# Edge layers of a graph network on one core: five more tiles fetched by indirect DMA, and twelve instead of six fetched tiles completed by VectorE

## The reference

```python
e = edge_attr @ We + be
m = jax.nn.relu(x[src] + e)
agg = jax.ops.segment_sum(m, dst, num_segments=x.shape[0])
h = ((1.0 + eps) * x + agg) @ W1 + b1
# batch norm over the nodes, relu
return jax.nn.relu(h @ W2 + b2)
```

## Time and profile before

| | |
|---|---|
| median of 3 runs | 876.57 us (871.54 to 879.27) |
| the profiled execution: its own time | 878.66 us |
| the profiled execution: its span, first to last instruction | 876.9 us |
| TensorE busy (matmul) | 786.6 us, 90% |
| VectorE busy | 697.3 us, 80% |
| ScalarE busy | 543.0 us, 62% |
| GpSimd busy | 283.1 us, 32% |
| mean granted TensorE clock | 0.965 |

### The profile page before, as it was taken

The page is one execution under the profiler, slowest core; times in us unless marked ns, Lnnn a source line. Parts: engine busy times, 40 slices in busy tenths (PEclk is TensorE's granted clock), DMA queues, the critical chain, the costliest instruction groups (busy, mean ns, idle before and its releaser), DMA issues.

```text
span 876.9 us, 12030 instructions
## 1 busy us (share of the span) xinstructions
PE 786.6 (90%) x3566; PEld 601.8 (69%) x3566; DVE 697.3 (80%) x1253; ACT 543.0 (62%) x1034; POOL 283.1 (32%) x230
## 2 busy tenths in 40 slices
PE   2979899899889899979999999988999989999895
PEld 2667565477467668756777777776777867878674
DVE  7989856799966968886798878977889778997635
ACT  2288213566563423556797778877788677864656
POOL 3000387877300000016760067400863028610000
PEclk9989999799989999997999999999999999999998
DMA  5323246788472330417994199823996249942001
GB/s 117 103 80 107 69 131 195 227 248 243 150 261 85 118 131 1 154 39 178 215 223 120 35 222 222 206 92 84 225 221 161 86 126 215 220 105 65 32 6 54
DMA packets 61329, 122.12 MB, mean 139 GB/s; under 512 B 9096, under 2 KB 22698, under 8 KB 61269
## 3 DMA queue, kind: packets, MB, share of 16 engines
q0 software_dynamic: 22096, 52.18, 27.2%
q1 hardware_dynamic: 39173, 69.17, 25.1%
HBM read 105.60 MB, written 15.73 MB: 138 GB/s over the span
## 4 chain that ended last, share of the span: by engine, by line
PE 59%; DVE 21%; ACT 11%; DMA 6%; issue 3%; SPq 0%; ACTq 0%; DVEq 0%
PE ps L712 12%; PE ps L1043 9%; PE ps L1082 6%; PE ps L1026 6%; PE ps L1067 6%; DVE z_parts L1955 5%; PE ps L820 5%; DMA onehot_dst<-onehot_rows 4%; PE ps L965 3%; PE ps L911 3%; DVE gathered_parts L1702 2%; DVE w L1462 2%; PE ps L704 2%; ACT slot_recs L1146 2%; ACT queued L1298 2%
## 5 line engine op out<-in xcount | busy, mean ns | idle before, releaser
L680 POOL DMA_INDIRECT queued<-node_rows,srci x92 | 144.4, 1569 | 198.3 <-DMA node_rows<-work 152.1
L1043 PE MATMUL ps<-z_parts,onehot_dst 128*125 128x512 f32 x664 | 189.4, 397 | 2.9 <-DMA onehot_dst<-onehot_rows 2.6
L1955 DVE SCALAR_TENSOR_TENSOR z_parts<-ps,z_parts 128x512 fp32r<-128x512 f32 x216 | 146.0, 689 | 34.5 <-ACT z_parts L1354 30.0
L712 PE MATMUL ps<-w,xT 128*125 128x512 f32 x660 | 169.2, 409 | 3.7 <-DVE w L1462 2.7
L1354 ACT ACTIVATE z_parts<-ps 128x512 fp32r<-128x512 f32 x216 | 128.1, 598 | 49.8 <-PE ps L1026 44.6
L712 PEld LDWEIGHTS ps<-w,xT 128*125 128x125 f32 x660 | 125.0, 193 | 35.1 <-issue 5.7
L1043 PEld LDWEIGHTS ps<-z_parts,onehot_dst 128*125 128x125 f32 x664 | 121.0, 186 | 39.9 <-issue 11.5
L1026 PE MATMUL ps<-x_parts,gather_lhs 128*128 x408 | 130.5, 401 | 5.1 <-DVE z_parts L1955 5.1
L1026 PEld LDWEIGHTS ps<-x_parts,gather_lhs 128*128 128x128 f32 x408 | 76.9, 189 | 26.0 <-issue 8.0
L674 POOL DMA_INDIRECT gathered<-rel_rows,rowi x75 | 77.8, 1037 | 22.8 <-issue 22.2
L1955 DVE SCALAR_TENSOR_TENSOR z_parts<-queued,z_parts 128x512 fp32r<-128x512 f32 x116 | 79.5, 685 | 5.8 <-ACT z_parts L1354 5.6
(11 more groups left out here) (285 smaller groups left out, 1125.8 us busy)
## 6 DMA issues: line engine op xcount, KB each, us to landing
w_stage<-in_weights SPq DMA_DIRECT2D x88, 256.0 KB, 3.8
onehot_dst<-onehot_rows SPq DMA_DIRECT2D x80, 250.0 KB, 5.1
onehot_rows<-onehot_dst SPq DMA_DIRECT2D x20, 250.0 KB, 2.4
gather_lhs<-edge_src_rows SPq DMA_DIRECT2D x8, 432.0 KB, 7.9
node_rows<-work SPq DMA_DIRECT2D x20, 160.0 KB, 2.0
queued<-node_rows,srci POOLq DMA_INDIRECT x116, 6.5
node_rows<-work SPq DMA_DIRECT2D x20, 90.0 KB, 2.0
rel_rows<-rel_rows_out SPq DMA_DIRECT2D x10, 160.0 KB, 1.9
```

Of the source, the lines that this page charges most:

```text
L680: gp.indirect_dma_start(Q[k % QR][:, :], None, xb_d, row, compute_op=ALU.add)\
L712: mm = pe.matmul(ps[0:R, bank, :], lt[:, a, k, n * R:(n + 1) * R], w[:, b, k, :], start=first and k == 0 and (a, b) == THREE[0], stop=last ...
L1043: mm = pe.matmul(psf[0:R, bass.ds(d, D)], S[:, j // SK % SR, j % SK, :], Z[:, g % ZR, a, :], start=False, stop=False, skip_group_check=True)
L1955: v.scalar_tensor_tensor(out=Z[:, g % ZR, LO, :], in0=of, scalar=0.0, in1=Z[:, g % ZR, HI, :].bitcast(F32), op0=ALU.max, op1=ALU.subtract) ...
```

## The change

Five full tiles of each layer, tiles 17, 26, 35, 44 and 53 (`EXTRA`; steps 21, 36, 51, 66 and 81), are no longer gathered by TensorE. They join the 29 rest tiles in the order of steps (`QT`, 34 entries), so GpSimd fetches them, and ten matmuls a layer at L1026 go. Their row numbers are made once per launch by four small VectorE instructions (`extra_rows`). Of the fetches from the 17th on, every third one is prefilled instead of every second one: 22 prefilled and 12 plain fetches a layer, hence 22 sets on ScalarE and 12 adds on VectorE. The 16 buffers are used in turn by all 34.

```diff
-SETS = QR + (TL - QR + 1) // 2
-ADDS = TL - SETS
+EXTRA = range(LEAD + 5, TF, 9)
+QT = [t for t in ORDER if t >= TF or t in EXTRA]
+QI = {t: k for k, t in enumerate(QT)}
+TQ = len(QT)
+GI = {t: i for i, t in enumerate(t for t in range(TF) if t not in EXTRA)}
+SETS = QR + -(-(TQ - QR) // 3)
+ADDS = TQ - SETS
...
         def prefilled(k):
-            return k < QR or (k - QR) % 2 == 0
+            return k < QR or (k - QR) % 3 == 0
+
+        def last_of(k):
+            return k % QR + (TQ - 1 - k % QR) // QR * QR
...
                 else:
-                    gp.wait_ge(z_made, l * TE + STEP[TF + k - QR] + 1)
+                    gp.wait_ge(z_made, l * TE + STEP[QT[k - QR]] + 1)
                     gp.indirect_dma_start(Q[k % QR][:, :], None, xb_d, row).then_inc(q_in[k % QR], 16)
...
+            gp.wait_ge(srcx_made, 1)
...
             for l in range(NL2):
                 gp.wait_ge(xb_out, 32 * NT * (l + 1))
-                for k in range(TL):
+                for k in range(TQ):
                     queue_rows(l, k)
...
-                    if 3 <= t < TF:
-                        s = src_at.of(t)
+                    s = src_at.of(t) if 3 <= t < TF else None
+                    if t in GI and t >= 3:
                         pe.wait_ge(z_made, l * TE + STEP[t - 3] + 1)
...
-                    while k < TL and STEP[TF + k] - 14 <= i:
+                    while k < TQ and STEP[QT[k]] - 14 <= i:
                         queue_set(l, k)
-                        k += 2
+                        k += 3
...
                 if l < NL2 - 1:
                     for k in range(SET_T):
-                        act.wait_ge(z_made, l * TE + STEP[TF + QR + k] + 1)
+                        act.wait_ge(z_made, l * TE + STEP[QT[last_of(k)]] + 1)
                         queue_set(l + 1, k)
...
+            def extra_rows():
+                of = rowf[:, EXTRA.start:EXTRA.stop:EXTRA.step]
+                link(v.tensor_scalar(srcx[:, :], of, float(N + 1), None, ALU.is_ge))
+                link(v.scalar_tensor_tensor(out=srcx[:, :], in0=of, scalar=float(2 * N + 1), in1=srcx[:, :],
+                                            op0=ALU.is_ge, op1=ALU.add))
+                link(v.scalar_tensor_tensor(out=srcx[:, :], in0=srcx[:, :], scalar=-float(N), in1=of,
+                                            op0=ALU.mult, op1=ALU.add))
+                v.tensor_scalar(srci[:, TL:TQ], srcx[:, :], -1.0, 0.0, ALU.add, ALU.max).then_inc(srcx_made, 1)
...
                 for i, t in enumerate(ORDER):
                     g = l * TE + i
-                    while k < TL and STEP[TF + k] <= i + 2:
-                        queue_add(l, k)
-                        k += 2
-                    of = ps[:, 5 + t % 3, :] if t < TF else Q[(t - TF) % QR][:, :]
+                    while k < TQ and STEP[QT[k]] <= i + 2:
+                        if not prefilled(k):
+                            queue_add(l, k)
+                        k += 1
+                    of = ps[:, 5 + t % 3, :] if t in GI else Q[QI[t] % QR][:, :]
```

More of the change, by code:

```diff
@@ L207, in build @@
         rowf = early("rowf", [P, TE])
+        srcx = early("srcx", [P, len(EXTRA)])
         nti = early("nti", [P, NT], I32)
@@ L273, in build @@
         besti, srcb, cword = topsi[:, 0, :], topsi[:, 1, :], topsi[:, 2, :]
-        srci = sb("srci", [P, TL], I32)
+        srci = sb("srci", [P, TQ], I32)
         dlo = sb("dlo", [P, TE])
@@ L336, in build @@
         rec_made = sem("records_made")
+        srcx_made = sem("rows_of_extra_tiles_made")
         rec_tr = sem("records_tr")
@@ L467, in queue_landed @@
             before = (TE - GA - 1 - k % QR) // GR + 1
-            return 16 * (before + l * ((TL - 1 - k % QR) // QR + 1) + k // QR + 1)
+            return 16 * (before + l * ((TQ - 1 - k % QR) // QR + 1) + k // QR + 1)
         @block.sync
@@ L676, in queue_rows @@
             def queue_rows(l, k):
-                row = bass.IndirectOffsetOnAxis(ap=srci[:, k:k + 1], axis=0)
+                c = QT[k] - TF if QT[k] >= TF else TL + EXTRA.index(QT[k])
+                row = bass.IndirectOffsetOnAxis(ap=srci[:, c:c + 1], axis=0)
                 if prefilled(k):
@@ L1296, in queue_set @@
                 if k >= QR:
-                    act.wait_ge(z_made, l * TE + STEP[TF + k - QR] + 1)
-                nc.scalar.activation(Q[k % QR][:, :], WEB[:, :], ACT.Copy, scale=wt[:, TF + k:TF + k + 1])\
+                    act.wait_ge(z_made, l * TE + STEP[QT[k - QR]] + 1)
+                nc.scalar.activation(Q[k % QR][:, :], WEB[:, :], ACT.Copy, scale=wt[:, QT[k]:QT[k] + 1])\
                     .then_inc(q_set, 1)
@@ L1342, in _ @@
                     g = l * TE + i
-                    if t < TF:
-                        act.wait_ge(gat_done, l * TF + t + 1)
+                    if t in GI:
+                        act.wait_ge(gat_done, l * len(GI) + GI[t] + 1)
                         of = ps[:, 5 + t % 3, :]
                     else:
-                        if prefilled(t - TF):
-                            act.wait_ge(q_in[(t - TF) % QR], queue_landed(l, t - TF))
-                        else:
-                            act.wait_ge(q_add, ADDS * l + adds(t - TF))
-                        of = Q[(t - TF) % QR][:, :]
+                        if prefilled(QI[t]):
+                            act.wait_ge(q_in[QI[t] % QR], queue_landed(l, QI[t]))
+                        else:
+                            act.wait_ge(q_add, ADDS * l + adds(QI[t]))
+                        of = Q[QI[t] % QR][:, :]
                     if g >= ZR:
@@ L1616, in _ @@
                                         op0=ALU.mult, op1=ALU.add))
-            v.tensor_scalar(srci[:, :], srcf[:, :], -1.0, 0.0, ALU.add, ALU.max)
+            v.tensor_scalar(srci[:, 0:TL], srcf[:, :], -1.0, 0.0, ALU.add, ALU.max)
             link(v.tensor_copy(wt[:, :], ps[:, 7, 2 * TE:3 * TE]))
             v.tensor_tensor(wt[:, :], wt[:, :], ps[:, 7, 3 * TE:4 * TE], ALU.add).then_inc(rec_made, 1)
+            def extra_rows():
[6 more added lines that the diff above has]
+                v.tensor_scalar(srci[:, TL:TQ], srcx[:, :], -1.0, 0.0, ALU.add, ALU.max).then_inc(srcx_made, 1)
             def count_onehots(g):
@@ L1651, in _ @@
                                     ALU.subtract).then_inc(rec_low, 1)
+                    extra_rows()
             for g in range(NCL):
@@ L1942, in queue_add @@
                 v.wait_ge(q_in[k % QR], queue_landed(l, k))
-                v.scalar_tensor_tensor(out=Q[k % QR][:, :], in0=WEB[:, :], scalar=wt[:, TF + k:TF + k + 1],
+                v.scalar_tensor_tensor(out=Q[k % QR][:, :], in0=WEB[:, :], scalar=wt[:, QT[k]:QT[k] + 1],
                                        in1=Q[k % QR][:, :], op0=ALU.mult, op1=ALU.add).then_inc(q_add, 1)
```

## The result

The changed kernel takes 900.46 us in the median of 4 runs (896.25 to 902.79), the kernel before 875.73 us beside it: ratio **1.0266**, 95% interval 1.0232 to 1.0300. Slower, as predicted; 894 us was forecast, with a range of 885 to 902. The measured median lies 1.5 us inside the upper end, and the kernel lost 24.7 us where 17.4 were forecast. The profiled execution has a span of 901.0 us (own time 902.79) against 876.9 us, 24.1 us more, where the prediction's sum was 17.0.

The account below looks back on a forecast made before the run. VectorE was taken to bound steps 48 to 82; 11.7 (layers) + 3.5 (between layers) + 0.8 (once per launch) + 1 (waits) = 17.0 us on the median of 876.57 gave 894 us, range 885 to 902.

Parts of the forecast that it names:

- The bound: Steps 48 to 82 of a layer: VectorE and TensorE level before; after the change VectorE is the bound by 4 us.
- VectorE's count: First add to last z of a layer: 12 adds, 34 z and 0.68 us make 29.0 us on VectorE.
- The matmuls saved: TensorE: ten gathers a layer go, 2.33 us, 9.3 over four layers; the three pairs behind step 48 give nothing.
- The late fetches: First add waits for the 18th fetch, landing 5.8 us after issue; with VectorE's count, +11.7 us over four layers.
- The 1 us that was left for VectorE's waits: About 1 us in all for VectorE waiting on ScalarE where a gathered, a fetched and an added tile meet.
- Between layers: Last add 1.2 us closer to the layer's end delays the next `We` and dense part: +3.5 us over three layers.
- Once per launch: Four small VectorE instructions while it makes one-hots for TensorE: 0 to +0.8 us, upper end taken.
- Fetches on time: Rival: first plain fetch lands before step 48 is due, VectorE's count remains: 9.5 us, 886 us; chance 0.17.
- DMA bound: Rival: one-hots take 7.3 us under fuller queues, 2.8 us a layer, 11 in all: 905 us; chance 0.10.
- TensorE decides: Rival: VectorE has slack for the adds in steps 48 to 82, 9.3 us come off: 867 us; chance 0.05 (faster).
- Adds block GpSimd: Rival: adds and fetch issues hold each other up, 24 us on top: 918 us; chance 0.03.
- The first add waits for a fetch: Sign to look for in the profile: VectorE's first add of a layer waits for a fetch; no size.

Follow-up runs that it names:

- adds9: Changed kernel with every second instead of every third fetch prefilled from the 17th on, 9 adds a layer: ratio 1.0115 to the kernel before.
- last_prefilled: Changed kernel with a layer's last two fetches prefilled instead of plain, 10 adds a layer: ratio 1.0050 to the kernel before.
- spread12: Changed kernel with its 12 plain fetches, and so its adds, spread over the first 29 of 34 fetches: ratio 1.0028 to the kernel before.
- after_again: Changed kernel unaltered, run on the second group's chip: 927.58 us, ratio 1.0158 to the kernel before.
- before_third: Kernel before with its own 29 fetched tiles, every third fetch prefilled from the 17th on, 8 adds instead of 6: ratio 1.0068 to the kernel before.
- late_extra: Changed kernel with its five moved tiles late in the layer (32, 37, 42, 47, 52): ratio 1.0219 to the kernel before.
- before_spread10: Kernel before with its 29 fetched tiles and 10 adds spread over the layer instead of 6 late ones: 872.95 us, ratio 0.9950.
- adds0: Changed kernel with all 34 fetches of a layer prefilled, no adds: ratio 1.0199 to the kernel before.
- adds18: Changed kernel with all 18 fetches from the 17th on plain, 18 adds a layer: ratio 1.0736 to the kernel before.

## Why the prediction was right, step by step, and what was mis-sized

**The bound** was read rightly. VectorE decides from step 48 on: 29.00 us busy in 29.00. `adds9`, `last_prefilled` and `spread12` have the changed kernel's matmuls and end at other times as their adds and fetches are placed.

**VectorE's count** is exact where nothing holds VectorE: 29.0 us forecast from first add to last z, 29.05 to 29.09 measured. On the second chip two layers of `after_again` took 1.0 and 1.7 us more, with an add waiting for its fetch in each. `before_third` shows the price of an add separately.

**The matmuls saved** brought nothing that shows, as said for the three pairs behind step 48. TensorE has 2.3 us of gaps in the stretch where it was full. In the first half it is busy 13.87 of 15.00 us instead of 14.75, and the bound stretch didn't start sooner for it. No run takes matmuls away and leaves the fetches as they are, so this is read from the timelines.

**The late fetches** were the right mechanism with the wrong fetch and too small a size. By the working of the prediction the first add was to start 44.2, 41.3, 41.2 and 42.0 us behind the layer's first matmul; it came at 44.90, 43.49, 42.26 and 43.12, 5.1 us later in sum. In layers 2 to 4 not the 18th fetch at 5.8 us but the 16th held the line, in layer 2 at 8.0 us. I had taken about the median landing of plain fetches (5.9); the earlier trace rows had prefilled ones of up to 7.6 us, the kernel before has one of 8.1 in its third layer, and they are needed first. Three of GpSimd's issues took 1.62 to 2.04 us instead of 1.54 besides. The 1 us that was left for VectorE's waits doesn't cover it. This term was 12.7 us and measured 17.0. `late_extra`, where the wait is gone in three layers, gets back 1.7 us: whether all of the 5.1 us are the fetches' is not shown.

**Between layers** 3.5 us were forecast and 5.8 measured. The dense part starts 6.34, 6.22 and 6.32 us behind the last z instead of 4.91, 4.90 and 4.93, 4.1 us in sum, near the forecast 1.2 us each, with 0.13 us more for the load of `We` (3.13 against 3.00 in the earlier trace rows). Another 1.7 us lie behind that start, 1.33 of them in layer 2. There TensorE's granted clock is the lower of its two levels, where it was the full one. The prediction had no term for it. The dense part's start before, then the stretch ahead of it and its start after, second layer:

```profile
576.30:579.00 2.70, 2.65 (x21) 2.67 (x21) 2.70 (x6) 2.70 (x6) 0.00 (x0) 1.00 0.00 0
```

```profile
584.20:589.20 5.00, 1.94 (x12) 1.25 (x12) 2.95 (x5) 4.63 (x9) 0.00 (x0) 0.87 0.00 0
589.20:592.80 3.60, 3.51 (x14) 3.51 (x15) 3.60 (x7) 3.60 (x7) 0.00 (x0) 0.50 0.00 0
```

TensorE was busy 1.94 of the 5.00 us ahead of it, with an idle of 2.41 us (1.09 before), and then works at 0.50, 1.2 GHz, until the clock comes back. In `last_prefilled`, with the chain out of the way, the same stretch has 1.00 in all three layers, and the time behind the start is 32.45 to 32.47 us instead of 33.78 in layer 2. Not every fall costs as much: in layer 3 the clock fell too, for 0.26 us more.

The long idle is not the only thing that goes with a fall. Over the profiled executions TensorE's idle just ahead of the dense part was 2.2 us or more in 14 of the layers 1 to 3, and the clock fell in all 14. But it fell in the kernel before as well, in layer 1 behind 1.13 us of idle, and in layer 3 of `before_spread10` behind 0.76 us:

```profile
471.66:474.36 2.70, 2.70 (x10) 2.70 (x11) 2.70 (x6) 2.70 (x6) 0.00 (x0) 0.50 0.02 6
675.44:678.14 2.70, 2.70 (x10) 2.70 (x11) 2.70 (x5) 2.70 (x6) 0.00 (x0) 0.50 0.00 0
```

With 0.76 to 1.42 us of idle, and the full clock until 0.5 us ahead of the start, it fell in 4 of 21 layers. In these executions the fall is rarer with the shorter chain, but not ruled out.

**Once per launch** 0.8 us were forecast and 1.4 measured, but two executions of the kernel before differ by 8 us in that place: it can't be told.

**The number.** The sum was 17.0 us and the profiled executions are 24.1 apart: 4.3 are missing in the layers, 2.3 between them and 0.6 ahead of them, all in one direction. That the time still fell into the range owes something to luck: the range's upper end took in part of the DMA rival, and that rival did not come true.

**The rivals.** *Fetches on time*: no layer of the changed kernel had it. Layers 2 to 4 of `late_extra` did, and they still take 3.6 to 4.6 us more than those of the kernel before. *DMA bound*: not in the changed kernel on the first chip. The one-hots land 5.4 us after issue in the median, and TensorE waited for them 1.5 us in the launch:

```profile
PE ps L1055 <- DMA onehot_dst<-onehot_rows: 1.5, 3, 0.8
```

It was 2.6 us before. On the second chip it was 6.1 us, and from the first edge matmul on that execution took 3.6 us longer; the waits for one-hots may be part of it. *TensorE decides*: fell. *Adds block GpSimd*: it fell as a cost. The 48 adds last 743 ns in the mean, as before, and GpSimd issues its last fetch 8 to 10 us ahead of a layer's end. But some issues did get longer: of the 15 prefilled issues with an add beside their first 0.94 us, 10 took over 1.61 us, and of the other 73 only 13 (9 of 14, and 14 of 74, in `after_again`). What lengthens them is not shown; `adds0`, without an add, has 22 such issues in 136. *The first add waits for a fetch*, named as a sign, was not to be seen in layer 2: the wait was one instruction earlier, on ScalarE.

**What remains open**: why the kernel before takes 912 to 916 us on two of the chips, and why it seems to lose more than the changed one there ahead of the edge layers; the stops in `adds18`; what makes the clock fall behind a short idle.

## What to carry to other kernels

Where two engines are level, count the instructions that a change gives to the other engine in the stretch where they will stand, not in the mean over the layer: twelve adds all behind step 48 cost 1.6%, the same twelve spread over the layer 0.3% on the same chip. Look at what the last instruction of a phase releases; moved 1.2 us closer to the end, it cost up to 2.7 us, in part because the next phase then started at a lower clock. Where fetches are close to late, cost each one that is needed ahead of the point in question, those of the slower kind too, and at their worst landing, not at the median. And before a ratio is put down to a change, see in which stage its microseconds lie.

## What the runs showed of the hardware

- A prefilled fetch (a DMA that adds) landed up to 8.0 us after its issue with a fetch issued every 1.84 us; all fetches of that layer lay between 4.5 and 8.0 us. In the kernel before's third layer it was 4.6 to 8.1 us.
- In the changed kernel's layer 2 the granted clock fell to 0.50 during 5.00 us in which TensorE was busy 1.94 us, the last 2.41 of them idle. In the kernel before's layer 2 it stayed at 1.00 with 1.09 us of idle, but in layer 1 it fell with 1.13.
- With plain fetches issued 1.25 us apart over 20 us, VectorE, ScalarE and TensorE stopped twice for about 4 us (`adds18`); with 12 plain ones between prefilled ones they did not.
- ScalarE's set behind a relu that waits for a landing can hold up the next fetch: two landings of 7.29 and 6.76 us stood in one layer's chain for that reason (`adds0`).
- The same program differs by 4% between chips (876 and 912 to 916 us), and a variant's ratio by 1 to 1.3% (1.0266 and 1.0158; 0.9973 and 0.9843): more than the intervals within one chip.
